# The order in which an instruction's semaphore waits are written, in a one-core kernel of convolution, attention and experts

## The reference

```python
# 1. convolution block
h = silu(conv1x1(group_norm(x, 32), w0, b0))              # group norm 1, conv0
y = silu(conv3x3(group_norm(h, 32), w1, b1, groups=4))    # group norm 2, conv1; 128 channels
y = group_norm(y, 2)                                      # group norm 3
a = y's mean over each 8x8 window, then the max over 2 radix halves
a = silu(conv1x1(a, w2, b2, groups=2))
a = group_norm(a, 8)                                      # the window norm, "gna"
a = softmax over the radix of conv1x1(a, w3, b3, groups=2)
o = weight @ (y gated by a)                               # sums over the radix halves
x = x + group_norm(o, 32)                                 # group norm 4
# 2. causal attention over the 16 images; a token is one pixel of one image
t = x as tokens (image, pixel, channel)
hn = layer_norm(t);  e = score_w . tanh(hn @ fc_w.T + fc_b)
t = t + softmax-weighted running sum of hn over the images up to this one
# 3. eight experts, mixed with one weight per pixel and expert
z = layer_norm(t);  r = softmax(mean over images of z @ Wr + br)
t = t + sum over e of r[e] * (relu(bn2(relu(bn1(z @ W1[e])) @ W2[e])) @ Wo[e] + bo[e])
```

## Time and profile before

| | |
|---|---|
| time, median of 3 runs | 140.77 us (140.62 to 140.92) |
| profiled execution: span, first to last instruction | 139.0 us |
| median less that span | 1.8 us |
| PE matmul busy | 120.3 us (87%), 891 instructions |
| DVE busy | 110.3 us (79%), 379 instructions |
| ACT busy | 79.8 us (57%), 172 instructions |
| POOL busy | 33.8 us (24%), 34 instructions |
| DMA, mean over the span | 36 GB/s |

### The profile page before, as it was taken

One profiled execution on the slowest core, in us unless ns is written; L12 is line 12 of the kernel. 1 busy time (PEld: TensorE's weight loads), 2 busy tenths in 40 slices (PEclk: granted clock), 3 DMA queues, 4 the chain that ended last, 5 costly groups with the idle time before them and its releaser, 6 DMA issues.

```text
span 139.0 us, 2634 instructions
## 1 busy us (share of the span) xinstructions
PE 120.3 (87%) x891; PEld 52.6 (38%) x891; DVE 110.3 (79%) x379; ACT 79.8 (57%) x172; POOL 33.8 (24%) x34
## 2 busy tenths in 40 slices
PE   6989699999973499899777899999699999999990
PEld 2333234443322363455264433544144542221320
DVE  0497878495588999999999999999775169999941
ACT  4003030399569859458454688789798994366300
POOL 8022362002503464246325062040130000000000
PEclk9999999999998556999999999999999999999999
DMA  4997000000000000000000000000000000020042
GB/s 81 386 419 194 0 2 5 0 0 5 0 2 5 0 0 2 0 0 0 0 5 0 0 0 2 5 0 0 0 0 5 0 0 0 5 78 2 0 151 75
DMA packets 2813, 4.96 MB, mean 36 GB/s; under 512 B 240, under 2 KB 2416, under 8 KB 2672
## 3 DMA queue, kind: packets, MB, share of 16 engines
q1 hardware_dynamic: 2656, 4.60, 9.5%
q10 hardware_dynamic: 144, 0.20, 0.8%
HBM read 3.75 MB, written 1.05 MB: 35 GB/s over the span
## 4 chain that ended last, share of the span: by engine, by line
PE 58%; DVE 31%; issue 4%; ACT 4%; POOL 2%; DVEq 0%; ACTq 0%; POOLq 0%
PE bank L1021 12%; PE bank L1008 12%; PE bank L1033 10%; PE bank L882 7%; PE bank L830 5%; DVE s_wst L602 4%; DVE y L654 3%; DVE hn L681 2%; DVE x L668 2%; PE bank L822 2%; PE bank L943 2%; DVE s_ln1sq L675 1%; ACT y L387 1%; PE bank L935 1%; PE bank L843 1%
## 5 line engine op out<-in xcount | busy, mean ns | idle before, releaser
L1008 PE MATMUL bank<-xs,f1s 64*64 64x512 f32 x128 | 19.6, 608 | 2.0 <-ACT h L446 1.2
L1021 PE MATMUL bank<-h,f2s 64*64 64x512 f32 x128 | 20.1, 604 | 0.0
L882 PE MATMUL bank<-pad,w 32*64 32x512 f32 x288 | 18.1, 598 | 0.3 <-DVE pad L560 0.3
L446 ACT ACTIVATE h<-bank,s_bnb 128x512 f32<-128x512 f32 x22 | 14.4, 687 | 5.0 <-PE bank L1008 5.0
L830 PE MATMUL bank<-warm 128*128 128x512 bf16 x32 | 10.3, 473 | 1.3 <-POOL warm L333 1.3
L359 ACT ACTIVATE act<-bank,par 128x512 f32<-128x512 f32 x4 | 2.7, 687 | 13.2 <-PE bank L843 13.1
L366 ACT ACTIVATE y<-bank,par 128x512 f32<-128x512 f32 x8 | 5.0, 681 | 8.9 <-PE bank L882 8.9
L882 PEld LDWEIGHTS bank<-pad,w 32*64 32x64 f32 x288 | 6.1, 130 | 7.4 <-issue 6.7
L1008 PEld LDWEIGHTS bank<-xs,f1s 64*64 64x64 f32 x128 | 5.2, 131 | 9.7 <-ACT h L446 4.8
L753 DVE TENSOR_SCALAR h<-bank,s_bnb 128x512 f32<-128x512 f32 x10 | 7.5, 746 | 1.4 <-PE bank L1008 1.4
L1021 PEld LDWEIGHTS bank<-h,f2s 64*64 64x64 f32 x128 | 5.5, 132 | 7.9 <-issue 3.9
(11 more groups left out here) (296 smaller groups left out, 261.7 us busy)
## 6 DMA issues: line engine op xcount, KB each, us to landing
par<-params SPq DMA_DIRECT2D x1, 1516.0 KB, 9.0
xin<-x SPq DMA_DIRECT2D x4, 256.0 KB, 4.5
out<-act SPq DMA_DIRECT2D x4, 256.0 KB, 2.1
row_par<-row_params SPq DMA_DIRECT2D x4, 160.0 KB, 8.8
w<-conv_w SPq DMA_DIRECT2D x1, 288.0 KB, 5.0
par<-params ACTq DMA_DIRECT2D x1, 193.5 KB, 4.0
```

The source lines that it names most:

```text
L446: A.activation(h1[n % 4][:], bank[Z1[h]][:], ACT.Relu, bias=tile("bnb", P, 3 * EP)[:, col:col + 1]).then_inc(h1_ready, 1)
L882: ins = T.matmul(bank[CONV1[k][2 * j + h]][at:at + C, :], w1[rows, tap, :], pad[rows, b:b + 2, dy:dy + S, dx:dx + S], start=(tap == 0), st ...
L1008: ins = T.matmul(bank[Z1[h]][to, :], f1s[own, e, to], xs[own, k], start=True, stop=True)
L1021: ins = T.matmul(bank[Z2[h]][at:at + C, :], f2s[rows, h, e, :], h1[n % 4][rows, :], start=True, stop=True)
```

## The change

Only the order of waits and one condition change; no instruction that computes, no buffer and nothing of the list is touched. `step` takes a second wait as an argument and writes it ahead of its own, so that at the 12 places `rstd_ready` is written first and `vector_done` second. On PE, `group_product`, `score`, `logits` and `weights_transposed` write the wait for their input first and the one for the free bank second. `conv1`, `to_tokens`, `x_transposes` and `layer2` swap theirs likewise. `layer1` waits for its relu first and for `xs_ready` only in the first unit of each quarter.

```diff
--- before.py
+++ after.py
@@ -475,10 +475,12 @@
         def _(dve):
             steps = [0]
 
-            def step(ins):
+            def step(ins, later=None):
 
                 steps[0] += 1
                 ins.then_inc(vector_done, 1)
+                if later is not None:
+                    dve.wait_ge(*later)
                 dve.wait_ge(vector_done, steps[0])
 
             V = nc.vector
@@ -497,10 +499,9 @@
                 step(V.scalar_tensor_tensor(sq, ms[:, 0, :], 1.0, ms[:, 0, :], ALU.mult, ALU.mult))
                 V.scalar_tensor_tensor(tile(t, rows, n), ms[:, 1, :], EPS, sq, ALU.add, ALU.subtract).then_inc(var_ready, 1)
 
-            def group_scale(name, n, rows=P):
-                t, _, _ = var_tiles[name]
-                dve.wait_ge(rstd_ready, VAR_AT[name])
-                return rstd(name), tile(t + "ms", rows, 2, n)[:, 0, :]
+            def rstd_of(name):
+
+                return rstd_ready, VAR_AT[name]
 
             def channel_means(name, n, sign):
                 t, _, _ = var_tiles[name]
@@ -540,8 +541,8 @@
 
             def normalise_x(k):
                 mean, ins = channel_means(("gn1", k), PK, 1.0)
-                step(ins)
-                r, _ = group_scale(("gn1", k), PK)
+                step(ins, rstd_of(("gn1", k)))
+                r = rstd(("gn1", k))
                 for i in range(PK):
                     V.tensor_scalar(xnorm[:, k * PK + i, :], xin[:, k * PK + i, :], mean[:, i:i + 1], r[:, i:i + 1],
                                     ALU.subtract, ALU.mult).then_inc(xnorm_ready, 1)
@@ -552,8 +553,8 @@
 
             def normalise_0(k):
                 mean, ins = channel_means(("gn2", k), PK, 1.0)
-                step(ins)
-                r, _ = group_scale(("gn2", k), PK)
+                step(ins, rstd_of(("gn2", k)))
+                r = rstd(("gn2", k))
                 dve.wait_ge(pads_zeroed, k + 1)
                 for i in range(PK):
                     b = k * PK + i
@@ -617,8 +618,9 @@
 
                 a = tile(f"win{k}", P, BQ, WIN)
                 mean = tile(f"gn3v{k}ms", P, 2, BQ)[:, 0, :]
-                step(V.scalar_tensor_tensor(a, tile(f"wmax{k}", P, BQ, WIN), 1.0 * WIN / PIX, each(mean, P, BQ, WIN), ALU.mult, ALU.subtract))
-                r, _ = group_scale(("gn3", k), BQ)
+                step(V.scalar_tensor_tensor(a, tile(f"wmax{k}", P, BQ, WIN), 1.0 * WIN / PIX, each(mean, P, BQ, WIN), ALU.mult, ALU.subtract),
+                     rstd_of(("gn3", k)))
+                r = rstd(("gn3", k))
                 V.tensor_tensor(a, a, each(r, P, BQ, WIN), ALU.mult).then_inc(stats_ready, 1)
                 V.scalar_tensor_tensor(tile(f"gn3v{k}nb", P, BQ), mean, -1.0, r, ALU.mult, ALU.mult).then_inc(gn3_shift_ready, 1)
 
@@ -639,8 +641,9 @@
             def window_normalise(k):
                 an = tile(f"wan{k}", C + 1, BQ, WIN)[0:C]
                 step(V.tensor_tensor(an, tile(f"wa{k}", C, 2, BQ * WIN)[:, 0, :].rearrange("p (b n) -> p b n", n=WIN),
-                                     each(tile(f"gnav{k}ms", C, 2, BQ)[:, 0, :], C, BQ, WIN), ALU.subtract))
-                r, _ = group_scale(("gna", k), BQ, C)
+                                     each(tile(f"gnav{k}ms", C, 2, BQ)[:, 0, :], C, BQ, WIN), ALU.subtract),
+                     rstd_of(("gna", k)))
+                r = rstd(("gna", k))
                 V.tensor_tensor(an, an, each(r, C, BQ, WIN), ALU.mult).then_inc(stats_ready, 1)
 
             def gate_y(k):
@@ -662,7 +665,8 @@
                 channel_means(("gn4", k), PQ, -1.0)[1].then_inc(gn4_mean_ready, 1)
 
             def residual1(k):
-                r, _ = group_scale(("gn4", k), PQ)
+                dve.wait_ge(*rstd_of(("gn4", k)))
+                r = rstd(("gn4", k))
                 for i in range(PQ):
                     dve.wait_ge(x_centred, PQ * k + i + 1)
                     V.scalar_tensor_tensor(x1[:, k * PQ + i, :], x1[:, k * PQ + i, :], r[:, i:i + 1], xin[:, k * PQ + i, :],
@@ -817,8 +821,8 @@
                     pe.wait_ge(small_free, SMALL_AT[name] - 1)
 
             def group_product(name, matrix, rhs, rows, n):
+                pe.wait_ge(stats_ready, STATS_AT[name])
                 small(name)
-                pe.wait_ge(stats_ready, STATS_AT[name])
                 T.matmul(bank[SMALL][0:rows, 0:n], matrix, rhs, start=True, stop=True).then_inc(small_ready, 1)
 
             def moments_product(name, matrix, n=PK):
@@ -867,10 +871,10 @@
 
                 k, tap = n // TAPS, n % TAPS
                 if tap == 0:
+                    pe.wait_ge(pad_ready, PK * (k + 1))
                     if k == 0:
                         pe.wait_ge(conv1_w_loaded, 16)
                         pe.wait_ge(act0_ready, 2)
-                    pe.wait_ge(pad_ready, PK * (k + 1))
                 dy, dx = tap // 3, tap % 3
                 for j in range(2):
                     b = k * PK + 2 * j
@@ -904,9 +908,10 @@
                 return x1[:, k * PQ + i, q * P:(q + 1) * P]
 
             def to_tokens(k):
-                pe.wait_ge(x_centred, PQ * (k + 1))
                 for i in range(PQ):
                     pe.wait_ge(x1_ready, PQ * k + i + 1)
+                    if i == 0:
+                        pe.wait_ge(x_centred, PQ * (k + 1))
                     for q in range(Q):
                         ins = T.matmul(block_of(k, q, i), x1_block(k, q, i), w("centre"), start=True, stop=True)
                 ins.then_inc(tok_in_psum, 1)
@@ -927,8 +932,8 @@
                 T.matmul(bank[CHAIN[k]][:], w("fc"), hch[:, k, :], start=True, stop=True).then_inc(fc_done, 1)
 
             def score(k):
+                pe.wait_ge(qch_ready, k + 1)
                 small(("score", k))
-                pe.wait_ge(qch_ready, k + 1)
                 for q in range(Q):
                     for i in range(PQ):
                         at, of = q * BQ + 2 * i, (q * PQ + i) * P
@@ -936,8 +941,8 @@
                 ins.then_inc(small_ready, 1)
 
             def x_transposes(k):
+                pe.wait_ge(xn2_ready, k + 1)
                 pe.wait_ge(qch_ready, k + 1)
-                pe.wait_ge(xn2_ready, k + 1)
                 for q in range(Q):
                     for i in range(PQ):
                         ins = T.transpose(block_of(k, q, i), pair_of(xn2, k, q, i), w("ident"))
@@ -961,15 +966,15 @@
                     ins.then_inc(ctx_turned, 1)
 
             def logits():
+                pe.wait_ge(xsum_ready, NQ)
                 small(("logits", 0))
-                pe.wait_ge(xsum_ready, NQ)
                 for q in range(Q):
                     ins = T.matmul(bank[SMALL][:, q * E:(q + 1) * E], tile(f"xsum{NQ - 1}", P, Q, P)[:, q, :], w("wr"), start=True, stop=True)
                 ins.then_inc(small_ready, 1)
 
             def weights_transposed():
+                pe.wait_ge(wt_ready, STRIPS)
                 small(("wt", 0))
-                pe.wait_ge(wt_ready, STRIPS)
                 T.transpose(bank[SMALL][:, 0:P], tile("wsoft", P, P), w("ident")).then_inc(small_ready, 1)
 
             def weights_spread():
@@ -995,13 +1000,14 @@
             def layer1(n):
                 k, e, h = units[n]
                 m = n // 2
+                if m:
+                    wait_relu1(m - 1, h)
+                if e == h == 0:
+                    pe.wait_ge(xs_ready, k + 1)
                 if n == 0:
                     pe.wait_ge(y_ready, 8)
                     pe.wait_ge(params_loaded, 16)
                     pe.wait_ge(small_free, SMALL_AT["s1row", 0])
-                elif m:
-                    wait_relu1(m - 1, h)
-                pe.wait_ge(xs_ready, k + 1)
                 own = slice(h * C, (h + 1) * C)
                 for j in range(2):
                     to = slice(j * C, (j + 1) * C)
@@ -1010,12 +1016,12 @@
 
             def layer2(n):
                 m, h, e = n // 2, n % 2, units[n][1]
+                if m:
+                    pe.wait_ge(h2_ready, n - 1)
+                wait_relu1(m, h)
                 if n == 0:
                     pe.wait_ge(ctx_added, 1)
                     pe.wait_ge(small_free, SMALL_AT["s2row", 0])
-                elif m:
-                    pe.wait_ge(h2_ready, n - 1)
-                wait_relu1(m, h)
                 for half in range(2):
                     rows, at = slice(half * C, (half + 1) * C), C * ((half + h) % 2)
                     ins = T.matmul(bank[Z2[h]][at:at + C, :], f2s[rows, h, e, :], h1[n % 4][rows, :], start=True, stop=True)
```

## The result

The changed kernel is slower: 141.69 us (median of 13 runs) against 140.92 (13 runs of the kernel before on the same chip), ratio 1.0069 with a 95% interval of 1.0042 to 1.0096. The forecast was 140.96 with a range of 140.5 to 141.25, so the result lies outside it. Measured again beside the last experiments it was 141.36 against 140.78, ratio 1.006 (1.0035 to 1.0084).

A forecast was written before the change was run, and what follows sets the result against it. DVE was taken to set the pace from 38.94 to 98.60 us and PE afterwards. Swap gains and losses summed to +0.21 less 0.02, or +0.19 us, on 140.77: 140.96 us, range 140.5 to 141.25.

The forecast's parts named there:

- Who comes last: 12 DVE pairs: POOL's result last in three, done first in nine; PE: mostly the input last, sometimes the bank.
- the price of each swap: Each swap: -0.06 us on PE or -0.07 on DVE if the last arrival moves first, the same loss otherwise.
- rival 2: PE's layers: dropping 28 separate waits frees its sequencer, perhaps 0.5 us, giving 140.3 us; chance 0.10.
- Rival 1: DVE steps: a wait on the own predecessor costs nothing wherever it stands; -0.26 us, 140.5 us; chance 0.14.
- s_wan 2: DVE pair near 52 us: a losing swap of 0.07 us, perhaps only 0.03 because its gap was already larger.
- The sum: Swap gains and losses added along the pace-setting engine, whole kernel: +0.19 us, 140.96 us; chance 0.58.
- Rival 3: Behind separate waits following instructions come late too, five DVE losses double: +0.54 us, 141.3 us; chance 0.18 including lower clock.
- the gate: DVE step at 38.68 us, waiting for ACT's s_wt, which hangs on PE's conv1: forecast 0.05 us early.
- the gn3 1 product's +0.06: PE product whose small bank DVE frees last, at 35.77 us: loses 0.06 us, and conv1 queues behind it.
- 45.14: DVE reduce released by PE's gn4 0 product, which goes from -0.05 to +0.01 us: running total +0.01 there.
- s_wan 1's 0.07: Losing DVE swap of 0.07 us, absorbed by the wait for PE's gn4 0 product before the reduce at 45.14.
- the square at 98.61: ACT step waiting for DVE's xc: DVE's delay passes through undiminished, making it 0.1 to 0.25 us late.

The follow-up runs named there:

- the second trace: Later profile of the unaltered changed kernel, taken with the last experiments: span 139.7 us; that kernel's repeated measurement 141.36 against 140.78 us for the kernel before.
- PE's half: Only PE's waits changed against the kernel before, DVE's pairs as before: 140.83 against 140.81 us, ratio 1.0006.
- the kernel with the last arrival first: Changed kernel with POOL's result first in only 3 of 12 DVE pairs, the free bank first for nine PE products: 140.49 against 140.75 us before.

## Why the prediction was wrong

**Who comes last, and the price of each swap: right.** In the second trace s_win 0 starts 0.03 us behind POOL's result in place of 0.10 (31.77 + 1.01 = 32.78 to 32.81; before 31.68 + 1.01 = 32.69 to 32.79), and the second half's xnorm 0.10 behind its mean in place of 0.03 (15.03 + 0.17 = 15.20 to 15.30), as the earlier trace rows had priced them. The separate waits are where they were forecast (by source line, first trace of the changed kernel; DVE's own step is line 484, layer 1's token wait 1006):

```profile
L484 DVEq EVENT_SEMAPHORE  x10: 21/21/21, 9.2 to 62.9; - x10
...
L1006 PEldq EVENT_SEMAPHORE  x3: 51/51/51, 89.4 to 111.5; - x3
```

That nine of twelve swaps put the wrong wait in front was the forecast's main claim, and the kernel that puts back those nine, and nine on PE, is faster than before. The 28 dropped waits of layer 1 gave nothing that PE's half could show, so rival 2 fell. Rival 1 fell too: a wait on the own predecessor does cost 0.07 us more when it is the separate one. What the Trainium skill's "VectorE: DVE Perf Modes" says in its section on the DRAIN, that a semaphore after each copy cost nothing extra, doesn't carry over to it: the gap is 0.10 us against 0.03 here.

**The step that failed: s_wan 2.** The sum had it at +0.03 to +0.07; in the second trace it is 0.66 less 0.25, +0.41 us. The row that gave it away was in the earlier trace rows, and I read it the wrong way round: I saw 0.07 us between 52.26 and 52.33 where every other such pair shows 0.03, and took it for a part of the loss already paid. It was the visible end of a 0.41 us bubble behind the separate wait at 51.9, and the change took its cover away. I should have asked where the odd gap begins and what hides the rest of it. Rival 3 came near in sign and kind ("the instructions that follow are taken in late too"), but put it on each of five places at 0.07 us, with 141.3 us; it is one place, at 0.4.

**A smaller miss: the gate.** Forecast 0.05 early, measured 0.13 less 0.03, 0.10 late. The sum carried the 0.13 us that s_win 0 and the w2 0 product gained through to the gate. In fact the sum at 34.88 (34.80 in the kernel before) waits for ACT's squares of y, and these come from conv1. ACT's last one there ends at 34.65 + 0.20 = 34.85 in the second trace, 34.77 in the kernel before:

```profile
34.65 0.20 ACT L374 ACTIVATION_READ_ACCUMULATOR more<-y 128x1 f32 x1
```

```profile
34.57 0.20 ACT L374 ACTIVATION_READ_ACCUMULATOR more<-y 128x1 f32 x1
```

So the start's +0.05 came back through PE and ACT, and the gn3 1 product's +0.06 added to it, since conv1 queues behind it. The price of the swap was right there, the path was not: DVE's gains ran into a wait that the sum had left out.

**And at 45.14.** Here the sum was right but for the gate. The reduce is released by PE's gn4 0 product, as forecast, and starts 0.04 us behind it:

```profile
44.72 0.57 PE L826 MATMUL bank<-s_gn4v0raw,par 128*128 128x12 f32 x2 [1.38 <-DVE s_gn3v2ms L497]
```

44.72 + 0.57 = 45.29, then 45.33; before 45.10, then 45.14. The product carries the gate's +0.10 and its own +0.06, the bank's release in the separate wait, in all +0.19 less 0.03, where +0.01 was forecast. s_wan 1's 0.07 fell into this wait, as forecast. From there to the square at 98.61 the forecast had +0.18 to +0.22, and measured are 0.77 less 0.19, +0.58; without the 0.34 to 0.38 that s_wan 2's step took beyond its term this is +0.20 to +0.24, as forecast. In sum, beyond the forecast +0.19: some 0.35 us from the bubble and 0.15 us from the gate, together the 0.7 us by which the second trace's span is longer.

**The range** was too narrow because the unexplained 0.04 us at s_wan 2 had no bound of their own. The chain of the kernel before shows the 0.41 us from 51.92 to 52.33. With these exposed the upper end would have been near 141.65 us (141.25 + 0.41), above the second measurement's 141.36 and just below the first series' 141.69, whose median includes the runs with the lower clock.

## What to carry to other kernels

Which of several waits rides on the instruction is worth 0.06 to 0.07 us a place, and only the arrival times of that place tell which it should be; a rule by kind ("the other engine's result comes last") was wrong in nine of twelve. Before moving a wait, look at what each gap around it covers: a gap that is a little longer than its kind is the tip of something that the neighbours hide. And when a small loss can't be placed, undo one site at a time and shift the instruction stream by a few instructions; if the loss moves with the numbering, it belongs to the stream, and the order of waits only decides whether it shows.

## What the runs showed of the hardware

- At one place of DVE's stream the instruction behind a separate wait starts 0.41 us after that wait is done, in place of 0.04 us. It was there in the kernel before, hidden (51.92 to 52.33), and in both traces of the changed one, open (52.57 to 52.99 in the second). It keeps its number in the stream: 27 more instructions ahead of it move it 27 instructions forward in the program.
- A second such place stands further on. Around 121 us DVE's sequencer runs through a row of separate waits, each done in 0.02 us, that start 0.10 to 0.11 us apart. Behind number 438 of DVE's recorded instructions the next one starts 0.47 us later in the kernel before (120.95, then 121.42). With 27 more instructions ahead the step is again behind number 438, now 113.44 to 113.90 us, and the row from 120.60 to 121.56 us has none. The separate waits in the 0.6 us from 120.9 us on in the kernel before, then from 113.4 us on in the kernel shifted by 27:

```profile
L781 DVEq EVENT_SEMAPHORE  x2: 21/21/21, 120.9 to 121.4; - x2
```

```profile
L787 DVEq EVENT_SEMAPHORE  x2: 21/21/21, 113.4 to 113.9; - x2
```

  The granted clock is 1.00 in both stretches, so PE's low clock isn't needed for it. It costs nothing there, since DVE is busy for all of the stretch from 121 to 122 us. Whether such places come at regular distances is open.
- The traces also have DMA packets of the kind "instruction". One of 8 KB starts 0.67 us after the step behind the bubble, and moves with it: at 53.66 in the second trace of the changed kernel (step at 52.99), at 53.00 in the kernel before (52.33), at 47.53 in the kernel shifted by 27 (46.86). Its bytes in 40 slices of 0.025 us, the second trace from 53 us on, then the kernel shifted by 27 from 47 us on:

```profile
GB/s 0 0 0 0 0 0 0 0 0 0 0 0 0 0 0 0 0 0 0 0 0 0 0 0 0 0 328 0 0 0 0 0 0 0 0 0 0 0 0 0
q14 instruction: 1, 0.01, 2.6%
```

```profile
GB/s 0 0 0 0 0 0 0 0 0 0 0 0 0 0 0 0 0 0 0 0 0 328 0 0 0 0 0 0 0 0 0 0 0 0 0 0 0 0 0 0
q14 instruction: 1, 0.01, 3.5%
```

  This ties the place to the way in which instructions are brought in. The packet starts behind the bubble, so it isn't what the step waited for; what that was, the traces don't show.
- The stretch at the low clock differs from run to run of one kernel; what decides it is not shown by any run here. In the traces of PE's half alone and of the kernel with the last arrival first a second, short stretch at the low clock fell at the start of the layers (76 to 84 us: clock 0.79 against 1.00, DVE busy 7.12 us against 7.79), and a relu that started at 80.80 in the kernel before started at 81.62 with PE's half alone, after 0.68 us of waiting for PE. The stretch of the kernel with the last arrival first, then the relu with PE's half alone:

```profile
76.00:84.00 8.00, 7.31 (x45) 3.04 (x45) 7.12 (x25) 4.46 (x9) 2.46 (x2) 0.79 0.00 0
```

```profile
81.62 0.75 DVE L753 TENSOR_SCALAR h<-bank,s_bnb 128x512 f32<-128x512 f32 x1 [0.68 <-PE bank L1010]
```

One trace of each kernel can't be compared there; many runs, sorted by their clocks, can.
